# An adaLN transformer block with linear attention on one core: a new order of work on all five engines, one tile of the first norm moved from GpSimd to ScalarE, and waits left out

## The chip, the core and the metric

The kernel runs on one core of a Trainium2 chip. Its time is the device time of one execution in microseconds; every time below is in microseconds unless marked ns. The engines are TensorE (PE in the profile, PEld for its weight loads), VectorE (DVE), ScalarE (ACT), GpSimd (POOL) and SyncE (SP), which here only issues DMAs.

## The reference

`x` has shape (8, 1024, 128). A condition gives for each of the 8 batches six rows of 128 numbers. The block is

```python
h = _layernorm(x) * (1 + ca) + sa
x = x + ga * attn(h, ...)          # 6 layers
h = _layernorm(x) * (1 + cb) + sb
x = x + gb * ffn(h, ...)           # fp4 quantised, inner width 352
```

Each of the six layers of `attn` does, with 8 heads of 16,

```python
xn = _layernorm(x, ln1_w[i], ln1_b[i])
q, k, v = xn @ wq[i], xn @ wk[i], xn @ wv[i]
q = softmax(q, axis=-1); k = softmax(k, axis=-2)     # k over the 1024 rows
context = einsum('bhnd,bhne->bhde', k, v)
x = einsum('bhnd,bhde->bhne', q, context) @ wo[i] + bo[i] + x
xn = _layernorm(x, ln2_w[i], ln2_b[i])
hdn = xn @ w1[i]                                     # 128 -> 512
x = where(hdn >= 0, hdn, 0.01 * hdn) @ w2[i] + x
```

`ffn` rounds its input, its hidden values and its weights to a grid of 4-bit floats in blocks of 16.

## The kernel before

An **item** is one batch in one layer: 48 items, batch by batch within a layer. An item is 1024 rows, held as 8 tiles of 128x128 (`T = 8`), all in SBUF. Every engine runs a hand-written order: a function `items(v)` lists steps such as `if on(v - 3): first_mlp(v - 3, 0)`, and is called for v = 0, 1, 2 and so on. The engines meet only through semaphores, so v on one engine is not the same time as v on another. A software pipeline results: while TensorE makes `product_k(v)`, it also works on the context of item v-1, the attention of v-2, and the MLP of v-3 to v-5.

The steps of one item, in the order of the data:

- `bn1_rows`, `moments1` (VectorE), `root1` (GpSimd) and `normalise1`: mean and variance of each row, then the normalised tiles. Of the 8 tiles GpSimd makes the first `POOL_TILES = 3` (L1758), ScalarE the other 5 (L861).
- `block_n` (VectorE, L1198) turns 32x32 squares; `send_n` and `fetch_n` (SyncE) move the squares through DRAM, which completes a transpose; `first_norm_t` (ScalarE, L817) applies the layer's scale. Item 0 (`FIRST_N = 1`) uses TensorE transposes in place of this way, and so do items 0 to 2 (`FIRST = 3`) for q and k.
- `product_k` (L556) writes the PSUM pair `S1`, `product_q` (L568) the pair `S0`, both fp32.
- `max_k`, `exp_k`, `block_k` (L1207), `send_k`, `fetch_k` for k; `max_q`, `shift_q`, `exp_q`, `sum_q`, `inverse_q`, `normalise_q` (GpSimd, L1791), `block_q` (L1184), `send_q`, `fetch_q` for q.
- `product_z` (L577, 16 fp32 instructions), `affine_z` (VectorE, L1228), `context` (L585, two instructions), `mask_context` (VectorE, L1233), `context_out` (L591, two), `bias_context` (VectorE, L1241), `attend` (L598, 16 fp32), `add_attention` (VectorE). Each of these waits for the one before it.
- `bn2_rows`, `moments2`, `root2`, `normalise2`, `second_norm_high`, `second_norm_low` (GpSimd): the second norm, split into two fp16 halves that a transposing DMA turns (`turn_hi`, `turn_lo`).
- `first_mlp(i, n)` for n = 0 to 7: three fp16 matmuls of 512 columns each (L612 to L614) into one of two PSUM banks in turn; `copy_hidden` (ScalarE, L880) empties the bank with the activation. `hidden_high` (ScalarE, L889) and `hidden_low` (GpSimd, L1785; for items 46 and 47 VectorE) split the hidden values.
- `second_mlp(i, t)` for t = 0 to 7: twelve fp16 matmuls of 128 columns each (L627 to L629); `add_mlp` (VectorE) adds the result to x.

In items 10 to 44 VectorE does one further step per v, `round_weights` or `prepare_gates`, for the feed-forward part at the end. That part works in 16 units of half a batch, in `ffn_phase(w)`; its first units are woven by hand into v = 48 to 53.

At the start the front norm of all batches (`front_stats`, `front_root`, `front_hat`, `front_rows`) and the splitting of the MLP weights (`prepare_weights`) are woven into v = 0 to 5, and TensorE runs filler matmuls (`keep_warm`, L522) between the products.

Of the kernel before, what the change touches and what calls it, by code (L numbers as in the profile page):

```python
# [37 lines left out]
def adaln_block(nc, x, ln1_w, ln1_b, wq, wk, wv, wo, bo, ln2_w, ln2_b, w1, w2,  # L38
# [23 lines left out]
    POOL_TILES = 3  # L62
    FIRST_N, FIRST = 1, 3
# [6 lines left out]
    with ctx:  # L70
# [208 lines left out]
        def _(sp):  # L279
# [169 lines left out]
        def _(pe):  # L449
# [110 lines left out]
            def product_q(i):  # L560

                pe.wait_ge(norm1_t_ready, i + 1)
                pe.wait_ge(wq_ready, 16 * (i // B + 1))
                after(pe, q_shifted, i)
# [16 lines left out]
            def context(i):  # L581
                pe.wait_ge(z_t_ready, i + 1)
                pe.wait_ge(wv_ready, 16 * (i // B + 1))
                w = wv_s[:, i // B % 2 * D:i // B % 2 * D + D]
                nc.tensor.matmul(S1[:, 0:D], w, z_t, start=True, stop=True).then_inc(ctx_done, 1)  # L585

            def context_out(i):
                pe.wait_ge(ctx_t_ready, i + 1)
                pe.wait_ge(wo_ready, 16 * (i // B + 1))
# [11 lines left out]
            def first_mlp(i, n):  # L601
# [14 lines left out]
            def second_mlp(i, t):  # L616
# [3 lines left out]
                if t % TH == 0:  # L620
                    pe.wait_ge(weights_ready, 2 * DEPTH)
# [39 lines left out]
            def product_gate(u, t):  # L661
                pe.wait_ge(f_x_q_t_ready, u + 1)
# [4 lines left out]
            def product_up(u, t):  # L667
                pe.wait_ge(f_x_q_t_ready, u + 1)
# [4 lines left out]
            def turn_hidden(u, t):  # L673
                if u == 0:
                    pe.wait_ge(x_ready, 2 * ITEMS - 1)
                pe.wait_ge(f_hid_q_ready, u + 1)
# [7 lines left out]
            def product_down(u):  # L684
# [3 lines left out]
                pe.wait_ge(f_x1_ready, u + 1)  # L688
# [29 lines left out]
            def items(v):  # L718
                if v == 0: turned_bias_rows()
                if v == 0: hidden_bias_cols()  # L720
                if v == 0: output_bias_rows()
                if v == 0: keep_warm(mlp0_bank, 18)
                if v == 0: turn_first_n(0)
                if on(v - 2): context_out(v - 2)
                if v == 2: keep_warm(mlp0_bank, 10)
                if v == 3: keep_warm(mlp0_bank, 16)
                if on(v - 4): first_mlp(v - 4, 6)
                if on(v - 4): first_mlp(v - 4, 7)
                if v == 51: product_gate(1, 0)
                if on(v - 2): attend(v - 2)  # L730
                if on(v - 5): second_mlp(v - 5, 5)
                if on(v - 5): second_mlp(v - 5, 6)
                if v == 50: turn_rows(0)
                if v == 52: turn_hidden(0, 0)
                if on(v): product_k(v)
                if v == 1: turn_first_k(0)
                if v == 3: turn_first_q(2)
                if on(v - 5): second_mlp(v - 5, 7)
                if v == 49: turn_weights()
# [4 lines left out]
                if v == 51: product_up(1, 1)  # L744
                if v == 51: product_gate(1, 2)
                if on(v): product_q(v)
                if v == 0: keep_warm(mlp0_bank, 30)
                if v == 0: prepare_bounds()
                if v == 0: keep_warm(S0, 14, q_shifted, 1)
                if v == 0: prepare_downs()  # L750
                if v == 1: keep_warm(mlp0_bank, 20)
                if v == 1: turn_first_q(0)
                if v == 2: keep_warm(mlp0_bank, 20)
                if v == 3: keep_warm(mlp0_bank, 14)
                if on(v - 3): first_mlp(v - 3, 0)
                if on(v - 3): first_mlp(v - 3, 1)
                if on(v - 4): second_mlp(v - 4, 0)
                if on(v - 3): first_mlp(v - 3, 2)
                if on(v - 3): first_mlp(v - 3, 3)
                if v == 50: product_gate(0, 1)  # L760
                if on(v - 4): second_mlp(v - 4, 1)
                if v == 51: product_up(1, 2)
                if on(v - 4): second_mlp(v - 4, 2)
                if on(v - 1): product_z(v - 1)
                if v == 1: turn_first_k(1)
                if v == 2: turn_first_q(1)
                if v == 1: keep_warm(mlp0_bank, 10)
# [1177 lines left out]
```

## Time and profile before

| | |
|---|---|
| runs | 1197.34, 1201.46, 1201.83; median 1201.46 |
| profiled execution | 1198.31, span 1196.6, mean granted TensorE clock 0.981 of full |
| TensorE busy | 1130.7 (94% of the span) |
| VectorE busy | 1074.4 (90%) |
| ScalarE busy | 1035.2 (87%) |
| GpSimd busy | 1091.4 (91%) |

The shares are over the whole span, of which some 120 us are the start, 830 us the items in their steady pace and 240 us the end. A matmul record ends later than the next begins, since matmuls are pipelined and their ends are modelled: distances between starts tell more than durations. Records of VectorE and ScalarE also overlap the next by some 0.1 us.

### The profile page before, as it was taken

How to read it: one execution, taken by the hardware profiler on the slowest of the kernel's cores; microseconds unless marked ns; L12 is line 12 of the kernel's file. 1: busy time of each engine (PE TensorE's matmuls, PEld its weight loads, DVE VectorE, ACT ScalarE, POOL GpSimd, SP SyncE). 2: the span in 40 equal slices, each digit the busy share in tenths (PEclk: the TensorE clock that was granted, in tenths of full speed). 3: DMA queues.
4: the chain of work that ended last, by engine and by line, in shares of the span. 5: the costliest groups of instructions: out<-in, count | busy, mean ns of one | idle time of the engine just before them, and what ended most of it. 6: DMA issues, size and time to landing. Idle time of an engine off the chain costs nothing.

```text
span 1196.6 us, 30119 instructions
## 1 busy us (share of the span) xinstructions
PE 1130.7 (94%) x9722; PEld 865.7 (72%) x9722; DVE 1074.4 (90%) x2885; ACT 1035.2 (87%) x1776; POOL 1091.4 (91%) x920
## 2 busy tenths in 40 slices
PE   7787999999999999999999999999999988999996
PEld 5575777777777777777778777777787755565664
DVE  7899989989999999999999999999987589999972
ACT  5687999999999999999999999999999886767662
POOL 4889999999999999999999999999999988999762
PEclk8798999999999999999999999999999999999998
DMA  8121877777667776687776776766777420110000
GB/s 308 36 71 53 234 187 224 195 195 223 193 195 214 196 216 194 180 224 187 216 201 197 216 206 183 221 190 204 208 193 218 108 71 18 36 37 36 18 19 36
DMA packets 213864, 190.22 MB, mean 159 GB/s; under 512 B 113392, under 2 KB 192080, under 8 KB 213712
## 3 DMA queue, kind: packets, MB, share of 16 engines
q1 hardware_dynamic: 213712, 188.31, 55.3%
q8 instruction: 81, 1.33, 0.5%
q14 instruction: 71, 0.58, 0.2%
HBM read 87.06 MB, written 76.02 MB: 136 GB/s over the span
## 4 chain that ended last, share of the span: by engine, by line
PE 50%; POOL 24%; issue 15%; DVE 6%; ACT 2%; DMA 1%; SPq 1%; DVEq 0%; POOLq 0%; ACTq 0%
POOL hidden L1785 10%; POOL rows_split L1777 4%; PE pair_mlp L556 4%; PE pair_mlp L577 4%; PE pair L598 4%; PE pair L568 4%; PE ring_pair L612 3%; PE ring_pair L614 3%; PE ring_pair L613 3%; PE mlp L696 3%; PE pair_mlp L670 3%; POOL arena L1758 2%; POOL arena L1791 2%; PE pair_mlp L681 2%; PE mlp L629 2%
## 5 line engine op out<-in xcount | busy, mean ns | idle before, releaser
L1785 POOL TENSOR_TENSOR hidden<-hidden 128x2048 f16<-128x2048 f32 x92 | 376.3, 4090 | 0.0
L880 ACT ACTIVATE hidden<-ring_pair,hidden_bias 128x512 f32<-128x512 f32 x384 | 245.6, 686 | 26.1 <-PE ring_pair L614 26.0
L889 ACT ACTIVATE hidden<-hidden 128x2048 f16<-128x2048 f32 x96 | 183.3, 1909 | 19.9 <-PE mlp L629 16.1
L1097 DVE BATCH_NORM_STATS2 bn<-x_all 128x6 f32<-128x128 f32 x896 | 184.2, 278 | 5.3 <-POOL x_all L1737 2.0
L1711 POOL TENSOR_TENSOR rstd<-ve,minus_half 128x8 f32<-128x8 f32 x104 | 170.7, 1641 | 0.0
L850 ACT ACTIVATE arena<-x_all,nmr,rstd 128x128 f32<-128x128 f32 x384 | 157.7, 494 | 0.0
L612 PE MATMUL ring_pair<-arena,halves 128*128 128x512 f16 x384 | 146.0, 380 | 3.4 <-ACT hidden L880 1.7
L614 PE MATMUL ring_pair<-arena,halves 128*128 128x512 f16 x384 | 146.0, 380 | 0.0
L613 PE MATMUL ring_pair<-arena,halves 128*128 128x512 f16 x384 | 146.0, 380 | 0.0
L627 PE MATMUL mlp<-halves,hidden 128*128 128x128 f16 x768 | 135.9, 219 | 1.4 <-issue 1.4
L627 PE MATMUL pair_mlp<-halves,hidden 128*128 128x128 f16 x768 | 136.0, 219 | 0.0
L628 PE MATMUL pair_mlp<-halves,hidden 128*128 128x128 f16 x768 | 136.0, 219 | 0.0
L629 PE MATMUL pair_mlp<-halves,hidden 128*128 128x128 f16 x768 | 136.0, 219 | 0.0
L629 PE MATMUL mlp<-halves,hidden 128*128 128x128 f16 x768 | 135.9, 219 | 0.0
L628 PE MATMUL mlp<-halves,hidden 128*128 128x128 f16 x768 | 135.9, 219 | 0.0
L1777 POOL TENSOR_TENSOR rows_split<-arena,rows_split 128x1024 f16<-128x1024 f32 x48 | 103.9, 2164 | 0.3 <-ACT rows_split L870 0.3
L598 PEld LDWEIGHTS pair<-small,arena 128*128 128x128 f32 x768 | 95.1, 195 | 10.6 <-DVE small L1241 4.2
L1791 POOL TENSOR_TENSOR arena<-arena,q_rec 128x1024 f32<-128x1024 f32 x48 | 93.9, 1956 | 6.9 <-DVE q_rec L1177 6.4
L598 PE MATMUL pair<-small,arena 128*128 128x128 f32 x768 | 95.9, 279 | 3.0 <-DVE small L1241 3.0
L861 ACT ACTIVATE arena<-x_all,nmr,rstd 128x128 f32<-128x128 f32 x240 | 97.8, 498 | 1.1 <-POOL nmr L1750 1.1
L556 PE MATMUL pair_mlp<-arena,layer_w 128*128 128x512 f32 x192 | 96.2, 624 | 1.4 <-ACT arena L811 1.4
L577 PE MATMUL pair_mlp<-arena 128*128 128x128 f32 x752 | 94.3, 279 | 3.0 <-DMA arena<-k_away 2.7
(206 smaller groups left out, 3144.5 us busy)
## 6 DMA issues: line engine op xcount, KB each, us to landing
n_away<-all_blocks SPq DMA_DIRECT2D x47, 512.0 KB, 3.0
norm_raw<-n_away SPq DMA_DIRECT2D x188, 128.0 KB, 3.2
k_away<-all_blocks SPq DMA_DIRECT2D x45, 512.0 KB, 2.8
q_away<-all_blocks SPq DMA_DIRECT2D x45, 512.0 KB, 3.3
arena<-k_away SPq DMA_DIRECT2D x180, 128.0 KB, 3.5
arena<-q_away SPq DMA_DIRECT2D x180, 128.0 KB, 3.6
x_all<-in_L_attn_x SPq DMA_DIRECT2D x8, 512.0 KB, 5.5
x_in<-in_L_attn_x SPq DMA_DIRECT2D x8, 512.0 KB, 4.0
```

The lines of the kernel that those rows point to most:

```text
L598: last = nc.tensor.matmul(tile(S0, t), tile(q_prob_t, t), ctx_o, start=True, stop=True)
L612: nc.tensor.matmul(ring[n % 2], hi, rows_hi, start=True, stop=False)
L613: nc.tensor.matmul(ring[n % 2], lo, rows_hi, start=False, stop=False)
L614: nc.tensor.matmul(ring[n % 2], hi, rows_lo, start=False, stop=True).then_inc(hidden_done, 1)
L627: nc.tensor.matmul(o, rows_hi, hi, start=(c == 0), stop=False)
L628: nc.tensor.matmul(o, rows_hi, lo, start=False, stop=False)
L629: last = nc.tensor.matmul(o, rows_lo, hi, start=False, stop=(c == HC - 1))
L880: act.activation(hidden_t[:, c * W + h * HALF:c * W + (h + 1) * HALF], ring[n % 2], ACT.Prelu, bias=hidden_bias[:, b:b + 1], scale=HIDDEN_ ...
L889: act.activation(half_rows(hidden_hi, h), half_rows(hidden_t, h), ACT.Copy).then_inc(hidden_hi_ready, 1)
L1097: last = nc.vector.bn_stats(bn[:, 6 * t:6 * t + 6], src(t))
L1711: return pool.tensor_tensor(rstd[:, 0:tiles], ve[:, 0:tiles], minus_half[:, 0:tiles], ALU.pow).then_inc(rstd_ready, 1)
L1785: pool.tensor_tensor(half_rows(hidden_lo, h), half_rows(hidden_t, h), half_rows(hidden_hi, h), ALU.subtract).then_inc(hidden_lo_ready, 1)
```

## The change

`POOL_TILES` goes from 3 to 2, so GpSimd normalises two tiles and ScalarE six. `FIRST` goes from 3 to 2: item 2's k and q go through DRAM. All `keep_warm` calls are dropped. The `items` orders of all five engines are new; in steady state `context_out` and `attend` of item v-1 now stand at the end of the same v. `second_norm_low` and `normalise_q` stand one v earlier at the end of GpSimd's order, `bn2_rows`, `add_attention` and `block_q` elsewhere in VectorE's, with `round_weights` and `prepare_gates` behind `bias_context`; `x_epsilon(4)`, `x_rows(6)` and `x_multiply(0)` change their place by a step or two. Waits that an earlier wait on the same engine already covers are left out. No instruction that computes is added or removed but those that follow from the two constants.

```diff
-    POOL_TILES = 3
-    FIRST_N, FIRST = 1, 3
+    POOL_TILES = 2
+    FIRST_N, FIRST = 1, 2
...
  SyncE
+                if on(v - 2): fetch_k(v - 2)
                 if on(v - 2): send_q(v - 2)
-                if on(v - 2): fetch_k(v - 2)
...
  waits, TensorE (those on VectorE, ScalarE and the other products alike)
                 pe.wait_ge(norm1_t_ready, i + 1)
-                pe.wait_ge(wk_ready, 16 * (i // B + 1))
+                if i % B == 0:
+                    pe.wait_ge(wk_ready, 16 * (i // B + 1))
...
-                after(pe, ctx_o_ready, i - 1)
...
-                pe.wait_ge(weights_ready, DEPTH)
-                pe.wait_ge(norm2_hi_ready, 16 * (i + 1))
-                pe.wait_ge(norm2_lo_ready, 16 * (i + 1))
+                if i == 0 and n == 0:
+                    pe.wait_ge(weights_ready, DEPTH)
+                if n == 0:
+                    pe.wait_ge(norm2_hi_ready, 16 * (i + 1))
+                    pe.wait_ge(norm2_lo_ready, 16 * (i + 1))
...
```

The steady part of the orders, each in one v (the steps of the start and of the end left out):

```
TensorE before: context_out(v-2)  first_mlp(v-4, 6 7)  attend(v-2)  second_mlp(v-5, 5 6)  product_k(v)
                second_mlp(v-5, 7)  product_q(v)  first_mlp(v-3, 0 1)  second_mlp(v-4, 0)  first_mlp(v-3, 2 3)
                second_mlp(v-4, 1 2)  product_z(v-1)  first_mlp(v-3, 4 5)  context(v-1)  second_mlp(v-4, 3 4)
TensorE after:  first_mlp(v-4, 6 7)  second_mlp(v-5, 4 5 6 7)  product_k(v)  first_mlp(v-3, 0)  product_q(v)
                first_mlp(v-3, 1)  second_mlp(v-4, 0 1)  first_mlp(v-3, 2)  product_z(v-1)  second_mlp(v-4, 2)
                first_mlp(v-3, 3)  context(v-1)  first_mlp(v-3, 4)  context_out(v-1)  second_mlp(v-4, 3)
                first_mlp(v-3, 5)  attend(v-1)

VectorE before: add_attention(v-4)  inverse_k(v-3)  bn2_rows(v-4)  moments2(v-4)  add_mlp(v-7,1)  max_k(v-2)
                block_n(v-1)  max_q(v-2)  shift_q(v-2)  bn1_rows(v)  moments1(v)  EXTRA STEP  affine_z(v-3)
                sum_q(v-2)  mask_context(v-3)  inverse_q(v-2)  bias_context(v-3)  block_k(v-2)  block_q(v-2)
                add_mlp(v-6,0)
VectorE after:  add_mlp(v-7,1)  block_q(v-3)  moments2(v-4)  max_k(v-2)  block_n(v-1)  max_q(v-2)  shift_q(v-2)
                bn1_rows(v)  affine_z(v-3)  moments1(v)  mask_context(v-3)  block_k(v-2)  bias_context(v-3)
                EXTRA STEP  inverse_k(v-2)  sum_q(v-2)  inverse_q(v-2)  add_attention(v-3)  add_mlp(v-6,0)
                bn2_rows(v-3)

ScalarE before: copy_hidden(v-5, 0 1)  exp_k(v-2)  copy_hidden(v-5, 2 3)  normalise2(v-4,0)  exp_q(v-2)
                normalise2(v-4,1)  copy_hidden(v-5, 4 5)  second_norm_high(v-4)  first_norm_t(v-1)
                hidden_high(v-5,0)  copy_hidden(v-5, 6 7)  normalise1(v)  hidden_high(v-5,1)
ScalarE after:  normalise2(v-4,0)  copy_hidden(v-5, 2)  normalise2(v-4,1)  copy_hidden(v-5, 3)
                second_norm_high(v-4)  exp_q(v-2)  copy_hidden(v-5, 4 5)  hidden_high(v-5,0)  copy_hidden(v-5, 6)
                first_norm_t(v-1)  copy_hidden(v-5, 7)  normalise1(v)  hidden_high(v-5,1)  copy_hidden(v-4, 0)
                exp_k(v-1)  copy_hidden(v-4, 1)

GpSimd before:  normalise_q(v-3)  second_norm_low(v-5)  normalise1(v-1)  hidden_low(v-6,0)  root2(v-4)
                hidden_low(v-6,1)  root1(v)
GpSimd after:   normalise1(v-1)  hidden_low(v-6,0)  root2(v-4)  hidden_low(v-6,1)  root1(v)
                second_norm_low(v-4)  normalise_q(v-2)
```

At the start `output_bias_rows` moves from ahead of `turn_first_n(0)` to behind `product_k(0)`, `fold_weights` on ScalarE from v = 0 to v = 1, `weight_bounds(0)` on VectorE from v = 1 to v = 2, and `prepare_scales` to a later place in v = 3.

## Rows read from the trace of the kernel before

**Rows 1.** Busy time by stretch: PE, PEld, DVE, ACT, POOL, PEclk, DMA share, GB/s.

```profile
100.00:150.00 50.00, 45.47 (x349) 33.64 (x348) 47.10 (x128) 42.89 (x71) 45.95 (x38) 0.90 0.58 163
...
300.00:500.00 200.00, 199.65 (x1908) 156.15 (x1906) 190.58 (x513) 190.82 (x304) 196.22 (x165) 1.00 0.71 201
```

**Rows 2.** Order of time, TensorE, product_k of items 5 and 47: start, length.

```profile
139.81 1.94 PE L556 MATMUL pair_mlp<-arena,layer_w 128*128 128x512 f32 x4
...
914.83 1.94 PE L556 MATMUL pair_mlp<-arena,layer_w 128*128 128x512 f32 x4
```

**Rows 3.** Order of time, TensorE, 519 to 528 us.

```profile
519.34 2.00 PE L577 MATMUL pair_mlp<-arena 128*128 128x128 f32 x16
521.18 0.38 PE L612 MATMUL ring_pair<-arena,halves 128*128 128x512 f16 x1
...
522.47 0.38 PE L585 MATMUL pair_mlp<-small,layer_w 128*128 128x128 f32 x2
522.69 0.22 PE L627 MATMUL pair_mlp<-halves,hidden 128*128 128x128 f16 x1
...
524.03 0.44 PE L591 MATMUL pair_mlp<-layer_w,small 128*128 128x128 f32 x2
524.31 0.38 PE L612 MATMUL ring_pair<-arena,halves 128*128 128x512 f16 x1
...
525.60 1.95 PE L598 MATMUL pair<-small,arena 128*128 128x128 f32 x16
527.39 0.22 PE L627 MATMUL mlp<-halves,hidden 128*128 128x128 f16 x1
```

**Rows 4.** Order of time, VectorE and one weight load, 502 to 527 us.

```profile
502.26 1.52 DVE L1421 TENSOR_TENSOR f_w<-f_w,x_in 128x560 f32<-128x560 f32 x1
503.70 0.34 DVE L1228 TENSOR_SCALAR small<-pair_mlp,ln_cols 128x128 f32<-128x128 f32 x1
...
504.09 0.30 PEld L585 LDWEIGHTS pair_mlp<-small,layer_w 128*128 128x128 f32 x2 [0.57 <-DVE small L1228]
...
520.88 1.18 DVE L1284 TENSOR_SCALAR x_in<-mod_out 128x512 f32<-128x512 f32 x1
521.98 0.34 DVE L1228 TENSOR_SCALAR small<-pair_mlp,ln_cols 128x128 f32<-128x128 f32 x1
...
524.51 0.35 DVE L1241 SCALAR_TENSOR_TENSOR small<-pair_mlp,cols,bo_rows 128x128 f32<-128x128 f32 x1 [0.41 <-PE pair_mlp L591]
524.78 1.23 DVE L1207 STREAM_TRANSPOSE all_blocks<-arena 128x1024 f32<-128x1024 f32 x1
526.15 1.25 DVE L1184 STREAM_TRANSPOSE all_blocks<-arena 128x1024 f32<-128x1024 f32 x1
```

**Rows 5.** Order of time, GpSimd: its three tiles of one first norm.

```profile
528.20 1.31 POOL L1758 TENSOR_SCALAR arena<-x_all,rstd,nmr 128x128 f32<-128x128 f32 x3
```

**Rows 6.** Order of time, ScalarE, 529 to 535 us.

```profile
529.24 2.05 ACT L861 ACTIVATE arena<-x_all,nmr,rstd 128x128 f32<-128x128 f32 x5
531.43 1.91 ACT L889 ACTIVATE hidden<-hidden 128x2048 f16<-128x2048 f32 x1
533.86 1.34 ACT L880 ACTIVATE hidden<-ring_pair,hidden_bias 128x512 f32<-128x512 f32 x2 [0.52 <-PE ring_pair L614]
```

**Rows 7.** DMAs of q: KB, median from issue to landing; four issues in time.

```profile
q_away<-all_blocks SPq DMA_DIRECT2D x45, 512.0 KB, 3.3
...
arena<-q_away SPq DMA_DIRECT2D x180, 128.0 KB, 3.6
...
516.76 2.15 SPq L352 DMA_DIRECT2D arena<-q_away  x4
```

**Rows 8.** Order of time, TensorE, product_k of item 1.

```profile
56.43 3.78 PE L556 MATMUL pair_mlp<-arena,layer_w 128*128 128x512 f32 x4
```

**Rows 9.** Order of time, the end of the items: SyncE and VectorE.

```profile
934.97 2.24 SPq L369 DMA_DIRECT2D arena<-k_away  x4
...
942.83 0.35 DVE L1228 TENSOR_SCALAR small<-pair_mlp,ln_cols 128x128 f32<-128x128 f32 x1 [5.78 <-PE pair_mlp L577]
```

More of the change, by code:

```diff
@@ L784, in items @@
                 if v == 51: product_gate(2, 0)
-                if v == 51: product_up(2, 0)
-                if v == 51: product_gate(2, 1)
+                if on(v - 3): first_mlp(v - 3, 2)
+                if on(v - 1): product_z(v - 1)
+                if on(v - 4): second_mlp(v - 4, 2)
+                if on(v - 3): first_mlp(v - 3, 3)
+                if v == 50: product_gate(0, 1)
+                if on(v - 1): context(v - 1)
+                if on(v - 3): first_mlp(v - 3, 4)
+                if on(v - 1): context_out(v - 1)
+                if on(v - 4): second_mlp(v - 4, 3)
+                if v == 50: product_up(0, 1)
+                if v == 50: product_gate(0, 2)
+                if on(v - 3): first_mlp(v - 3, 5)
+                if on(v - 1): attend(v - 1)
             for v in range(ITEMS + 5):
@@ L875, in copy_hidden @@
                 act.wait_ge(hidden_done, PIECES * i + n + 1)
-                act.wait_ge(scales_ready, 1)
+                if i == 0 and n == 0:
+                    act.wait_ge(scales_ready, 1)
                 if c == 0:
@@ L1598, in items @@
                 if v == 53: hidden_max(1)
+                if on(v - 3): block_q(v - 3)
+                if on(v - 4): moments2(v - 4)
+                if v == 51: x_scaled(0)
+                if v == 51: x_shifted(0)
+                if v == 51: x_moments(2)
+                if v == 51: x_max(0)
+                if v == 51: x_scale(0)
+                if v == 51: x_inverse(0)
+                if v == 51: x_lift(0)
+                if v == 51: x_lower(0)
                 if on(v - 2): max_k(v - 2)
+                if v == 2: weight_bounds(0)
                 if v == 2: output_bias()
-                if v == 49: x_rows(1)
-                if v == 49: x_moments(1)
                 if on(v - 1): block_n(v - 1)
                 if on(v - 2): max_q(v - 2)
+                if v == 4: prepare_weights(0, range(0, 3))
+                if v == 5: prepare_weights(1, range(0, 3))
+                if on(v - 2): shift_q(v - 2)
+                if v == 48: x_rows(0)
+                if v == 49: x_rows(1)
+                if on(v): bn1_rows(v)
                 if v == 2: prepare_bounds()
-                if on(v - 2): shift_q(v - 2)
-                if on(v): bn1_rows(v)
-                if v == 2: front_stats(4)
-                if v == 5: prepare_weights(1, range(0, 3))
+                if on(v - 3): affine_z(v - 3)
                 if on(v): moments1(v)
@@ L1879, in items @@
                 if v == 0: front_root(1)
-                if on(v - 3): normalise_q(v - 3)
-                if v == 4: front_root(6)
-                if on(v - 5): second_norm_low(v - 5)
-                if v == 49: gate(1)
                 if on(v - 1): normalise1(v - 1)
@@ L1909, in items @@
                 if v == 51: x_divide(0)
+                if on(v - 6): hidden_low(v - 6, 1)
+                if v == 48: gate(1)
+                if v == 49: gate(2)
+                if v == 51: x_multiply(0)
                 if on(v): root1(v)
-                if v == 2: front_root(4)
+                if v == 3: front_root(5)
+                if v == 3: front_rows(4)
+                if on(v - 4): second_norm_low(v - 4)
+                if v == 47: gate(0)
+                if v == 50: x_root(1)
+                if on(v - 2): normalise_q(v - 2)
                 if v == 4: front_root(7)
@@ L1915, in _ @@
                 items(v)
-            x_multiply(0)
             x_root(2)
```

244 lines of the change are left out of this document (101 added, 143 removed).

## The prediction

> **What bounds the kernel now.** I read the busy time by stretch first, then the order of time of each engine over one item in the middle, then the start and the end. Between 300 and 500 us the fp32 and fp16 products keep TensorE busy 199.65 of 200 us at full clock, GpSimd 196.2, ScalarE 190.8, VectorE 190.6 [rows 1]: four engines within 5% of one another, so none can be read as the bound from its share. The pace is in the starts of `product_k`: item 5 starts at 139.81, item 47 at 914.83 [rows 2], 42 intervals of 18.45 us. These 775 us are two thirds of the span of 1196.6.
>
> One item on TensorE [rows 3]: the records tell starts well, ends less well, so I cost a group by the distance to the next group's start. `product_z` stands behind a `second_mlp` tile and takes 521.18 - 519.34 = 1.84. `attend`, 16 fp32 instructions like it, stands behind a `first_mlp` group and takes 527.39 - 525.60 = 1.79. `context` behind `first_mlp` takes 0.22, its twin `context_out` behind `second_mlp` 0.28. An fp32 group that starts behind a 128-column product so costs about 0.055 us more than one behind a 512-column product, once per group. Two `first_mlp` groups lie between `context_out` and `attend`: 525.60 - 524.31 = 1.29, 0.645 each; two `second_mlp` tiles between `context` and `context_out`: 524.03 - 522.69 = 1.34, 0.67 each. `product_k` I take at 1.94 less the 0.16 by which such records reach into the next group (2.00 for 1.84 of `product_z`): 1.78 [rows 2, 3]. One item is then 8 x 0.645 + 8 x 0.67 + 1.78 + 1.84 (k, q) + 1.84 + 1.79 (z, `attend`) + 0.22 + 0.28 = 18.27. So TensorE's own work is 18.27 of 18.45, TensorE is the bound, and the 0.18 above it in the mean are stalls. One is seen whole [rows 4]: a `round_weights` step of 1.52 us on VectorE stands ahead of `affine_z` (L1228), which starts at 503.70 where a shorter step (item after) lets it start early enough; TensorE's weight load for `context` then sits idle 0.57.
>
> **The change part by part.** (1) *TensorE's order.* In steady state `product_q` moves from behind `second_mlp` 7 to behind `first_mlp` 0, `product_z` from behind `second_mlp` 2 to behind `first_mlp` 2, `context_out` from behind `second_mlp` 4 to behind `first_mlp` 4. `product_k` stays behind a `second_mlp` tile, `context` and `attend` behind `first_mlp`. 3 x 0.055 = 0.17, floor 18.27 - 0.17 = 18.10.
>
> (2) *First norm.* GpSimd gives up one of three tiles: 1.31 us for three [rows 5], so 0.44 less. It was busy 98% of the time [rows 1]; what it needs falls to about 17.6. ScalarE gets it: five tiles in 2.05 [rows 6], 0.41 more at most. In a period of 18.27 ScalarE waits 0.24 behind the five tiles (531.43 less 529.24 less 1.95, its records overlapping by 0.1) and 0.62 ahead of 533.86 (1.81 after 531.43) [rows 6]: work 17.4, new 17.8. That fits under 18.10 with 0.3 over.
>
> (3) *VectorE's order.* Between two `affine_z` (503.70 and 521.98) lie 18.28 us, of which 0.42 wait for `context_out` (like the 0.41 in front of 524.51), 0.14 for q's probabilities (as between 524.78 with its 1.23 and 526.15), and 1.10 are an extra step (1.18 less the overlap of 0.08) [rows 4]: work 16.6. With an extra step, 17.7; with the longest (1.52, 1.44 net), 18.05. The extra step moves from ahead of `affine_z` to behind `bias_context`, where nothing on TensorE waits for it at once. So the stall of rows 4 has no cause left, and even the longest step fits, with 0.05 to spare.
>
> (4) *What comes close.* `context` to `context_out` had 1.34 us of `second_mlp` between, now one `first_mlp`: 0.22 + 0.645 = 0.87 from start to start. In this time `context` must end, `mask_context` run and the weights be loaded. The record of 504.09 says how fast that goes: `affine_z` starts 503.70 and the weight load starts 0.39 later; a group whose load was late begins about 0.11 later in effect; and VectorE's answer to a finished pair comes 0.42 after its start (524.03 to 524.51, less 0.06 for standing behind a short product) [rows 3, 4]. `mask_context` is 0.06 shorter than `affine_z`, so 0.33. Sum 0.42 + 0.33 + 0.11 = 0.86 against 0.87: no stall if VectorE is already waiting, which it is when its extra step is short; a stall of its lateness otherwise. From `context` to `attend` there are 0.87 + 0.22 + 0.67 + 0.645 = 2.40; needed are 0.42, the mask 0.20, `block_k` 1.15 (1.23 less the overlap), `bias_context` to the load 0.40, and 0.11: 2.28. I take 0.05 per item for both: 18.15. Bounds: 18.10, and 18.35 if each long step costs what it cost before.
>
> (5) *DMA and SyncE.* `fetch_k` now goes out ahead of `send_q`, `normalise_q` follows the sum directly, `block_q` comes after the two additions, and ends some 9.9 us behind `mask_context`'s start (an estimate: the 17.7 of work less 7.8 for the steps from `moments2` to `moments1`). Then `q_away` 3.3, four fetches issued in 2.15, the last 1.6 after the first, and 3.6 to land [rows 7]: 9.9 + 3.3 + 1.6 + 3.6 = 18.4, and `attend` of this item comes 20.1 behind that mask (a period and the 2.40 less 0.42 of the last part). 1.7 over at medians. `send_n` and the two turns of the second norm follow `block_n`, `second_norm_high` and `second_norm_low` as before, and these keep their distance to their users to within a microsecond. Worth 0; if the cover goes, `attend` waits, and half of each us comes on every item, since the loop spans two.
>
> (6) *Implied waits* on all engines: passed waits cost nothing that shows; `first_mlp` has four of them and starts on the beat [rows 3]. Worth 0.
>
> Steady part: 42 x (18.45 - 18.15) = 12.6 us gained; at 18.10, 14.7; at 18.35, 4.2.
>
> (7) *The start.* All 172 filler products go, item 2 takes the DMA way (one `copy_k`, one `copy_q` less on ScalarE, two VectorE transposes of 1.16 more), the output bias rows move behind `product_k(0)`. VectorE is busy 47.1 of 50 us here [rows 1], so it is the bound and its 2.3 more count, at most 2.9 per 50 us of idle can be saved. Clock: `product_k(1)`, after a pause of TensorE, took 3.78 for what takes 1.94 later [rows 2, 8]: 1.2 instead of 2.4 GHz. Without fillers more groups do so. What VectorE waits for directly (`context`, `context_out`, `attend`) is 2.4 us more per item at half clock; three items, 7 us, if nothing hides it; hidden it is 0. On the other side the work ahead of `product_k(0)` shrinks by about 6. I take +2, bounds -4 and +8. The Trainium skill (TensorE: Matmul & The Clock Gate, section "Why this matters for your kernels") says that a pause between bursts of matmuls puts the engine back to half clock; by that rule all of items 0 to 3 are at half clock, which is my third rival below, and the row of `product_k(1)` agrees with it, since even with fillers it fell.
>
> (8) *The end.* From item 47 on VectorE stands 5.78 us in front of `affine_z(47)`, because `fetch_k` went out at 934.97, behind `send_q` [rows 9]. Now `block_k(47)` is ahead of `bias_context` and `fetch_k` ahead of `send_q`; then `product_z(47)` no longer has to wait for `block_q`, the two turns and `send_q` to be issued; I put that at 3 us. What follows, 16 equal units of the feed-forward part, is not touched. I take -3, bounds -6 and +4, as VectorE's hand order of the last items is changed throughout.
>
> Sum: -12.6 + 2 - 3 = -13.6. The profiled execution took 1198.3 us (span 1196.6 and 1.7 around it): 1184.7. The median of the runs is 3.2 above it, which gives 1187.9, so 1188.
>
> **The rivals.** (a) *VectorE becomes the bound.* It has 0.05 over in long steps; with 0.3 more per item (waits, or slower neighbours) the period is 18.35 and the sum is -4.2 - 1 = -5: 1196. For it: 35 of the 42 items have an extra step. Against: the step stands where it blocks nothing. (b) *ScalarE becomes the bound.* It now needs 17.8; if it keeps waiting 0.86 per item as before, the period is 18.6, 42 x 0.2 = 7 slower, less 1: 1207. It decides from waits of 0.65 on. Against: its waits were slack from TensorE's pace and shrink with it. (c) *The start at half clock.* All four 1.8 us groups and the two small ones double: 7.8 per item, 23 for three, if TensorE is the chain; then -15.6 + 23 = +7: 1209, slower by over 0.5% from 22 us on and no gain from 16. Against: VectorE, not TensorE, fills that time. (d) *All goes well:* 18.10, start 0, end -6: -21, 1180. (e) The reorder does nothing, since the tail of 0.055 comes from modelled ends: the starts do not depend on these; then 18.32 and 1195, counted with (a).
>
> **How the numbers follow.** My forecast 0.62 (own range 1182 to 1194), (a) with (e) 0.16, (b) 0.06, (c) 0.08, (d) 0.08. A measurement of this kernel tells 0.5%, 6 us, from no change. Faster by more (under 1195.5): forecast, (d), a third of (a): 0.75. Within 0.5%: the rest of (a), half of (c): 0.15. Slower: (b), the rest of (c): 0.10. The range 1178 to 1203 leaves out the best tenth-part of (d) and (b) with the end of (c).
>
> **What would show it.** Starts of `product_k` 18.1 to 18.2 apart with all 42 alike; `product_q` and `product_z` 1.79 instead of 1.84; no wait of TensorE for L1228; GpSimd under 98%, ScalarE at 98%. Wrong would be: waits of TensorE for `mask_context` or `bias_context` of over 0.1 per item, ScalarE without gaps at 18.3 or more, `product_k(4)` much later than 121.95, or the first unit of the feed-forward part later against item 47 than now.

## The result and the profile after

The changed kernel takes 1205.17 us, median of 7 runs (1201.43 to 1205.8), the kernel before 1200.92 beside it on the same chip. The ratio is 1.0039, with an interval of 1.0026 to 1.0052: slower by 4 us (0.4%), not faster by 13. The forecast of 1188 was wrong, and 1205.17 lies above the range of 1178 to 1203.

The head of the page of the changed kernel, its busy time between 300 and 500 us, and the starts of `product_k` of items 5 and 47 answer to [rows 1, 2]:

```profile
span 1199.6 us, 28217 instructions
PE 1108.4 (92%) x9534; PEld 851.3 (71%) x9534; DVE 1049.0 (87%) x2887; ACT 1045.5 (87%) x1822; POOL 1069.8 (89%) x872
```
```profile
300.00:500.00 200.00, 196.26 (x1903) 156.09 (x1902) 182.53 (x511) 193.26 (x314) 192.56 (x152) 1.00 0.71 202
```
```profile
141.37 1.98 PE L556 MATMUL pair_mlp<-arena,layer_w 128*128 128x512 f32 x4
...
919.19 1.94 PE L556 MATMUL pair_mlp<-arena,layer_w 128*128 128x512 f32 x4
```

TensorE has gone from 199.65 busy us in 200 to 196.26, VectorE and GpSimd have lost share as well, and only ScalarE, which got a tile, has gained. TensorE is still the busiest, but now it also stands still at times. The span divides so: up to `product_k(5)` 1.6 more than before (141.37 against 139.81; the forecast had +2), from item 47 on 1.4 less (280.4 against 281.8; the forecast had -3), and the 42 intervals between, which were to give 12.6, take 777.8 instead of 775.0.

Within these intervals the forecast's floor is there: most are 18.11 long (18.10 was worked out), so in most items TensorE still sets the pace. But some are 18.6 to 19.9. Added up over the groups of TensorE, stalls between items 5 and 47 are 17.5 us, against 7.4 to 8.1 before. Where they stand is in the list of waits between 200 and 914 us (engine and line, what it waited for: total, times, longest; L615 is the first product of `first_mlp`, L576 `product_z`):

```profile
PEld ring_pair L615 <- issue: 24.2, 33, 2.4
...
PEld ring_pair L615 <- DMA arena<-rows_split: 9.9, 5, 2.1
...
PEld pair_mlp L576 <- DMA arena<-k_away: 2.8, 3, 1.2
```

Most of the 24.2 us of the first row lie below a `product_k` that still runs and cost nothing: a weight load that waits is a stall only where the products behind it start late. Group by group, 10.9 of the 17.5 us stand ahead of `first_mlp` 0 (8 items, at most 1.79), 3.0 ahead of `product_z`, 2.4 ahead of `attend`. Nothing of this was in the list of what would make the forecast wrong: these are waits for DMAs. The transfers out of `rows_split` are the two turned halves of the second norm, which `turn_hi` and `turn_lo` bring. What the SyncE queue waited for most, first in the changed kernel, then in the one before, 200 to 914 us:

```profile
SPq L80 <- PE ring_pair L617: 131.5, 38, 3.8
```
```profile
SPq L360 <- DVE all_blocks L1207: 172.1, 39, 5.4
```

The wait of the first view has no row in the kernel before. L80 is the helper `after`, and L617 is the last product of a `first_mlp` piece, the one that counts `hidden_done`. In the code, which the change leaves alone here:

```
def turn_hi(i):
    sp.wait_ge(rows_hi_ready, i + 1)
    after(sp, hidden_done, PIECES * i)
    sp.dma_start(norm2_hi.rearrange(...), rows_hi, transpose=True).then_inc(norm2_hi_ready, 16)
```

There is one buffer of the turned norm. Item i may be turned into it only when `first_mlp` 7 of item i-1 has read it. Before the change SyncE never waited for this: it was held up by `send_k`, which waits for `block_k`, and when that had gone the buffer was free, though not for long: `turn_hi` goes out 0.7 us behind the end of `first_mlp` 7 in nearly every item. Here is one item of before, the last product of `first_mlp` 7, `product_k` and the first product of the next `first_mlp` 0 on TensorE, then SyncE:

```profile
507.12 0.38 PE L614 MATMUL ring_pair<-arena,halves 128*128 128x512 f16 x1
510.45 1.94 PE L556 MATMUL pair_mlp<-arena,layer_w 128*128 128x512 f32 x4
514.74 0.38 PE L612 MATMUL ring_pair<-arena,halves 128*128 128x512 f16 x1
...
507.77 0.34 SPq L360 DMA_DIRECT2D k_away<-all_blocks  x1
508.20 1.41 SPq L331 DMA_TRANSPOSE arena<-rows_split  x1
509.96 1.23 SPq L336 DMA_TRANSPOSE arena<-rows_split  x1
```

And two items of the changed kernel, with the same three places on TensorE, one on the beat and one that stalls:

```profile
655.73 0.38 PE L617 MATMUL ring_pair<-arena,halves 128*128 128x512 f16 x1
658.63 1.94 PE L556 MATMUL pair_mlp<-arena,layer_w 128*128 128x512 f32 x4
660.40 0.38 PE L615 MATMUL ring_pair<-arena,halves 128*128 128x512 f16 x1
...
673.84 0.38 PE L617 MATMUL ring_pair<-arena,halves 128*128 128x512 f16 x1
676.74 1.94 PE L556 MATMUL pair_mlp<-arena,layer_w 128*128 128x512 f32 x4
680.04 0.38 PE L615 MATMUL ring_pair<-arena,halves 128*128 128x512 f16 x1 [1.37 <-issue]
```
```profile
652.35 0.34 SPq L360 DMA_DIRECT2D k_away<-all_blocks  x1
656.19 1.23 SPq L331 DMA_TRANSPOSE arena<-rows_split  x1
657.51 1.26 SPq L336 DMA_TRANSPOSE arena<-rows_split  x1
658.87 1.95 SPq L369 DMA_DIRECT2D arena<-k_away  x4
...
674.31 1.23 SPq L331 DMA_TRANSPOSE arena<-rows_split  x1
675.96 2.05 SPq L336 DMA_TRANSPOSE arena<-rows_split  x1
```

From the end of `first_mlp` 7 to the start of the next `first_mlp` 0 there were 514.74 - 507.50 = 7.2 us. Now there are 660.40 - 656.11 = 4.3, since `attend` and `product_q` (1.79 and 1.84) no longer lie between, and one more `second_mlp` tile (0.67) does. Into the gap must go: the release (0.1), `turn_hi` at the queue (1.32 from issue to issue), and the landing of `turn_lo`, 2.8 at the median. That is 4.2 of 4.3. It fits at the median, and each longer landing (they run to 4.5) or second issue (675.96, 1.65 behind the first) stops TensorE. The long ones are no plain scatter. The eight items that stall stand five apart (6, 11, 16 and so on to 41), and in each of the eight a transfer of the queue that the page calls instruction (q8, 16 KB each) starts 0.97 to 2.28 us behind the issue of `turn_hi`; in the other 34 of items 2 to 43 none starts between that issue and the landing of `turn_lo`. That the one delays the other is a guess from this coincidence, and no run tried it. `fetch_k` stands behind both turns in the queue and so is late for `product_z`. The DMAs themselves have not slowed: the two turns landed in 3.5 and 2.9 us at the median before, in 2.7 and 2.8 after. The Trainium skill (DMA: Bandwidth & Descriptors, section "Anatomy of one DMA — SWDGE (gpsimd) path") says of the DMA engines that they do not wait on semaphores, and that such a wait is spent on the issuing sequencer before dispatch. The row of 131.5 us, on the queue of SyncE, agrees, and it is why the wait also delays what stands behind.

### The profile page after: what moved, and what is told of

It reads as the page before. It is cut to its first block, busy times and chain, and to the rows that moved or that the text cites. A ratio compares the mean times of both kernels' runs of the same rounds, so it can differ in the third digit from the quotient of the medians.

```text
span 1199.6 us, 28217 instructions
## 1 busy us (share of the span) xinstructions
PE 1108.4 (92%) x9534; PEld 851.3 (71%) x9534; DVE 1049.0 (87%) x2887; ACT 1045.5 (87%) x1822; POOL 1069.8 (89%) x872
## 4 chain that ended last, share of the span: by engine, by line
POOL 48%; issue 30%; DVE 13%; PE 7%; ACT 1%; DMA 0%; POOLq 0%; DVEq 0%; SPq 0%; ACTq 0%
POOL hidden L1773 28%; POOL rows_split L1765 9%; POOL arena L1746 3%; DVE ring_pair L1357 2%; DVE arena L1494 2%; PE pair_mlp L674 1%; DVE arena L1375 1%; POOL arena L1779 1%; DVE bn L1086 1%; PE mlp L700 1%; DVE arena L1372 1%; POOL shift L1754 1%; POOL ve L1753 1%; PE mlp L510 1%; POOL nmr L1760 1%
## 5 line engine op out<-in xcount | busy, mean ns | idle before, releaser
L871 ACT ACTIVATE hidden<-ring_pair,hidden_bias 128x512 f32<-128x512 f32 x384 | 257.8, 686 | 34.2 <-PE ring_pair L617 31.4
L615 PE MATMUL ring_pair<-arena,halves 128*128 128x512 f16 x384 | 146.0, 380 | 20.1 <-issue 10.0
L840 ACT ACTIVATE arena<-x_all,nmr,rstd 128x128 f32<-128x128 f32 x384 | 158.7, 499 | 5.4 <-POOL nmr L1760 5.3
L617 PE MATMUL ring_pair<-arena,halves 128*128 128x512 f16 x384 | 146.0, 380 | 0.0
L633 PE MATMUL mlp<-halves,hidden 128*128 128x128 f16 x768 | 131.3, 219 | 0.0
L631 PE MATMUL mlp<-halves,hidden 128*128 128x128 f16 x768 | 131.3, 219 | 0.0
L632 PE MATMUL mlp<-halves,hidden 128*128 128x128 f16 x768 | 131.3, 219 | 0.0
L851 ACT ACTIVATE arena<-x_all,nmr,rstd 128x128 f32<-128x128 f32 x288 | 116.0, 496 | 0.0
L1765 POOL TENSOR_TENSOR rows_split<-arena,rows_split 128x1024 f16<-128x1024 f32 x48 | 113.7, 2368 | 0.0
L599 PE MATMUL pair<-small,arena 128*128 128x128 f32 x768 | 98.4, 283 | 4.2 <-DVE small L1230 2.6
L576 PEld LDWEIGHTS pair_mlp<-arena 128*128 128x128 f32 x752 | 90.7, 192 | 13.2 <-DMA arena<-k_away 4.5
```

Source lines behind the costliest of these rows:

```text
L599: last = nc.tensor.matmul(tile(S0, t), tile(q_prob_t, t), ctx_o, start=True, stop=True)
L615: nc.tensor.matmul(ring[n % 2], hi, rows_hi, start=True, stop=False)
L631: nc.tensor.matmul(o, rows_hi, hi, start=(c == 0), stop=False)
L632: nc.tensor.matmul(o, rows_hi, lo, start=False, stop=False)
L633: last = nc.tensor.matmul(o, rows_lo, hi, start=False, stop=(c == HC - 1))
L840: last = act.activation(tile(norm2, t), x_all[:, bass.ds((i % B) * W + t * D, D)], ACT.Identity, scale=rstd2[:, t:t + 1], bias=nmr2[:, t:t ...
```

## The experiments

The theory: the wait for the single buffer, in a gap cut from 7.2 to 4.3 us, makes the stalls. The kernels ran in four sessions, each beside the kernel before, whose medians were 1199.0, 1200.1, 1200.8 and 1199.3. The times are medians; ratios are to the kernel before.

**A second buffer.** Item i then waits only for `first_mlp` 7 of item i-2:

```
+ norm2_more = sb("norm2_more", W)
- after(sp, hidden_done, PIECES * i)
+ after(sp, hidden_done, PIECES * (i - 1))     # and norm2_hi[i % 2], norm2_lo[i % 2]
```

> The changed kernel with a second buffer for the turned halves of the second norm, so that turn_hi and turn_lo of an item no longer wait for first_mlp 7 of the item before; nothing else differs. Theory 1 (the new TensorE order leaves only 4.4 us between the end of first_mlp 7 and the start of first_mlp 0 of the next item, and two transposing DMAs have to be issued and land in it): the 10.9 us of waits ahead of first_mlp 0 go, and the waits for k (3.0 us) too, because fetch_k behind the two turns is issued some 2 us earlier; about 14 us less than the changed kernel, 1191, 0.8% under the kernel before. Theory 2 (DMAs land later in this order because the queues are fuller, wherever they are issued): the waits move to other users and at least two thirds of the 17.5 us stay, 1200 to 1205.

Measured: 1184.6 us (1184.35 to 1185.94), ratio 0.988 [0.986, 0.990]. In its trace (one line is added, so 557 is 556 of before) `product_k` and the turns stand so:

```profile
142.15 1.98 PE L557 MATMUL pair_mlp<-arena,layer_w 128*128 128x512 f32 x4
903.63 1.94 PE L557 MATMUL pair_mlp<-arena,layer_w 128*128 128x512 f32 x4
...
607.03 0.34 SPq L361 DMA_DIRECT2D k_away<-all_blocks  x1
607.47 1.53 SPq L332 DMA_TRANSPOSE arena<-rows_split  x1
609.59 1.23 SPq L337 DMA_TRANSPOSE arena<-rows_split  x1
...
615.08 0.38 PE L616 MATMUL ring_pair<-arena,halves 128*128 128x512 f16 x1
```

SyncE's wait for L618 (617 of the changed kernel) is 0.4 us in all instead of 131.5. `turn_lo` goes out 5.5 us ahead of its reader, and the steady part is 903.63 - 142.15 = 761.5 us: 42 intervals of 18.13. This is the forecast's own steady part (18.15), and 1184.6 is inside its range.

**The same buffer in the old order**, as a control:

> The kernel before with the second buffer for the turned second norm, nothing else: the control for the two_buffers run. Theory 1 (the buffer matters only since the new order brought first_mlp 7 and the next first_mlp 0 close): in the kernel before some 7.4 us lie between the two and nothing waited there after the start, so within 0.3% of the kernel before, 1196 to 1202. Rival (the buffer helps any order, for instance since SyncE's later fetches go out earlier, so the change gave nothing): most of the 1.2% that two_buffers gained, 1186 to 1190.

Measured: 1200.4 us, ratio 1.001 [0.999, 1.002]. The buffer is worth nothing where the gap is 7.2 us. So it is not a gain in itself; the new order made it short.

**A longer gap instead of a buffer:** `product_q` ahead of `first_mlp` 0.

```
+ if on(v): product_q(v)
  if on(v - 3): first_mlp(v - 3, 0)
- if on(v): product_q(v)
```

> The changed kernel with product_q ahead of first_mlp 0 instead of behind it, one swap in TensorE's order. Theory 1: first_mlp 0 comes 1.8 us later against the turns, more than the longest stall seen there (1.79), so 10.9 us of waits go; product_q stands behind a second_mlp tile again and costs 0.055 us more per item, 2.3 us. Sum 8.6 us less than the changed kernel, 1196.5, 0.35% under the kernel before; the period without a stall is 18.16. If the waits ahead of first_mlp 0 are not for the turns: no gain, 1207.

Measured: 1194.6 us (1192.36 to 1198.2), ratio 0.996 [0.995, 0.997]. `first_mlp` 0 stalls 0.7 us in place of 10.9, but `product_z` now 6.8 in place of 3.0, because the turns still wait for the buffer (132.3 us) and `fetch_k` stands behind them. The interval stays 18.11: I had expected 18.16, but `product_q` stands behind `product_k` here, with 512 columns, and not behind a short product.

**The first norm's tile alone**, in the old order (`POOL_TILES = 2`), and given back in the new one (`POOL_TILES = 3`):

> The kernel before with two tiles of the first norm on GpSimd and six on ScalarE, nothing else. If TensorE's own 18.27 us per item bound the kernel before: within 0.2% of it, 1199 to 1203. If GpSimd, on which the chain that ended last ran up to about 480 us, set the pace there: up to 0.44 us less for some 18 items, 8 us less, 1193. If ScalarE has no room for the tile: up to 0.4 us more per item, 17 us, 1218.

> The changed kernel with three tiles of the first norm on GpSimd and five on ScalarE, nothing else. GpSimd's work is then 17.6 + 0.44 = 18.0 us for a period of 18.11, and it waits about 0.3 per item for q's reciprocals: if the moved tile is needed for the new pace, the period without a stall rises to some 18.3 and the time by about 8 us, to 1213. If GpSimd's waits are slack, the period stays 18.11 and the time within 2 us of the changed kernel's 1205.

Measured: 1195.3 us (ratio 0.997 [0.996, 0.998]) and 1205.3 us (1.005 [1.003, 1.007]). In the old order the tile takes the stalls around `context` (3.8 us) and 1.9 of the 2.8 in front of `product_z`: the interval is 18.27 almost throughout, 1.5 to 2.1 us of stalls are left, and the steady part is 6.1 us shorter (the start 1.9 longer). The time lies between the first two cases, since both hold in part: TensorE bounds, at 18.27, and the stalls above that were GpSimd's lateness. VectorE hands it on, though its list of waits between 200 and 910 us has none for GpSimd. The step of [rows 4] that took 1.52 us at 502.26 is the same instruction that takes 0.77 with two tiles. First GpSimd beside it in the kernel before, then GpSimd and VectorE with two tiles:

```profile
499.09 4.10 POOL L1785 TENSOR_TENSOR hidden<-hidden 128x2048 f16<-128x2048 f32 x1
```
```profile
496.45 4.08 POOL L1785 TENSOR_TENSOR hidden<-hidden 128x2048 f16<-128x2048 f32 x1
500.36 0.77 DVE L1421 TENSOR_TENSOR f_w<-f_w,x_in 128x560 f32<-128x560 f32 x1
501.05 0.34 DVE L1228 TENSOR_SCALAR small<-pair_mlp,ln_cols 128x128 f32<-128x128 f32 x1
```

Before, `hidden_low` on GpSimd ends at 503.2, 0.9 us behind the start of VectorE's step; with two tiles it ends 0.2 behind it. In both the step ends some 0.6 behind that end, and `affine_z` (L1228) follows. So GpSimd, earlier by the tile, lets go of VectorE's extra steps earlier: those of 128x512 or 128x560 elements took 0.98 to 1.52 us before and take 0.39 to 0.88 here, but for the reductions, 0.70 in both. In the changed kernel giving the tile back costs no more than its runs spread.

**With two buffers, the parts of the forecast one at a time.** First `product_z` back behind a 128-column product (`second_mlp` 2 ahead of it):

> The two_buffers kernel with product_z behind second_mlp 2 instead of ahead of it, so that its first fp32 weight load stands behind a 128-column product. If the tail is what the order gained: product_z takes 1.84 instead of 1.79, the period goes from 18.11 to 18.16 or 18.17, 2.3 us more in 42 items, 1187. If the place behind a short or a long product costs nothing: 18.11 and 1184.6.

Measured: 1189.4 us, ratio 0.992 [0.990, 0.993], 4.8 more than two buffers alone, twice what was expected (4.2 more in the steady part of the traces). Each interval is 18.23 instead of 18.11:

```profile
404.67 2.00 PE L577 MATMUL pair_mlp<-arena 128*128 128x128 f32 x16
406.51 0.38 PE L616 MATMUL ring_pair<-arena,halves 128*128 128x512 f16 x1
...
407.12 0.30 PEld L586 LDWEIGHTS pair_mlp<-small,layer_w 128*128 128x128 f32 x2 [0.29 <-DVE small L1217]
407.16 0.45 PE L586 MATMUL pair_mlp<-small,layer_w 128*128 128x128 f32 x2
407.45 0.38 PE L616 MATMUL ring_pair<-arena,halves 128*128 128x512 f16 x1
```

`product_z` takes 1.84 (1.78 to 1.79 with two buffers), the 0.055 of the forecast. The other 0.07 is at `context`, 0.29 instead of 0.22: only `first_mlp` 3 is left between the two, and `affine_z` comes 0.1 late. The term was right, and the swap made a wait beside it.

Then 172 fillers at the start again (the expectation says 178; the edit has 172, as many as before), in the places where the new order has its pauses, and all waits that the change had left out:

> The two_buffers kernel with 178 filler products at the start again, near their places of before. If the half clock at the start costs time (rival c of the prediction, 16 to 23 us, or my own 2): product_k of item 5 starts 2 to 8 us earlier than the 142.15 of two_buffers and the whole is that much shorter, 1177 to 1182. If VectorE and GpSimd fill that time anyway: product_k of item 5 within 1 us, 1184 to 1186.

> The two_buffers kernel with all the waits that the change left out as implied put back, on TensorE, ScalarE and VectorE. Passed waits cost nothing: period 18.11, 1184 to 1186. If each costs some tens of ns of a queue: first_mlp has up to three more per group and TensorE is at its floor, so the period would rise by 0.1 to 0.5 us, 4 to 20 us in all.

Measured: 1184.8 us (1183.83 to 1185.47) with the fillers, no different; `product_k(5)` starts 0.6 earlier. The granted clock did go up, as the busy time from 50 to 100 us shows, first without and then with them (the clock is the number behind POOL's):

```profile
50.00:100.00 50.00, 33.63 (x151) 26.03 (x150) 48.72 (x161) 39.30 (x76) 36.83 (x43) 0.67 0.28 81
```
```profile
50.00:100.00 50.00, 36.29 (x247) 29.70 (x248) 47.76 (x171) 38.91 (x74) 37.16 (x41) 0.87 0.26 76
```

VectorE is busy 48.7 of the 50 us in the one and 47.8 in the other: it sets this stretch, whatever the clock. With the waits back 1187.2 us (1187.12 to 1187.47), 2.6 more, above the 1184 to 1186 of the first case. Its steady part is 761.2 us, as without them, `product_k(5)` is 0.4 later and the stretch behind item 47 1.1 longer. So passed waits cost nothing per item, and a little at the ends; why there, no run shows.

**The queue order of SyncE.** If the turns must wait, can `fetch_k` go ahead of them?

```
- if on(v - 2): fetch_k(v - 2)     (first in the item)
  if on(v - 1): send_k(v - 1)
+ if on(v - 1): fetch_k(v - 1)
  if on(v - 3): turn_hi(v - 3)
```

> The changed kernel with one line of SyncE's order moved: the fetch of the k blocks stands behind its own send, ahead of the two turns of the second norm, instead of behind them. In the kernel with product_q ahead of first_mlp 0 the send went out at 596.10 and the turns at 599.93, so the fetch should go out near 598.5 and be on the queue for 2 us, and the turns, which wait for first_mlp 7, lose nothing. Theory (both waits have the turns' buffer as their source: first_mlp 0 waits for the landing itself, product_z for what stands behind the turns in the queue): product_z's stalls (3.0 us between 158 and 914) go, those of first_mlp 0 (10.9 us) stay, so about 1202 us. Rival (the DMA engines are simply more loaded): both stay, 1205 us, or the sum moves from one to the other.

> product_q ahead of first_mlp 0 on TensorE, and the fetch of the k blocks ahead of the two turns on SyncE; still one buffer of the turned second norm. Theory: the first half took 10 us of first_mlp 0's stalls and left 6.8 us at product_z, because the fetch stands behind the turns; with the fetch ahead, those go too and only attend's wait for the q blocks is left: 1187 to 1189 us, without the second buffer. Rival (the stalls are of the load of the DMA engines, and move to whichever user is next): 1193 to 1196 us.

Measured: 1262.3 us (ratio 1.052 [1.050, 1.054]) and 1198.5 us (0.998 [0.997, 1.000]). Both missed, the first by 60 us, and the second is no better than the swap of `product_q` alone (0.996). Its chain of work that ended last, over one item:

```profile
576.45 3.20 DMA arena<-rows_split
579.65 1.08 issue
580.73 0.38 PE ring_pair L615
...
589.06 0.23 PE pair_mlp L585 x2
589.32 0.07 DVE small L1221
...
589.53 1.25 DVE all_blocks L1195
590.79 3.42 DMA k_away<-all_blocks
594.23 0.30 SPq L369
...
595.52 0.43 SPq L369
596.05 3.26 DMA arena<-rows_split
```

This is a ring. The turn lands, `first_mlp` 0 and the products up to `context` run, `mask_context` and `block_k` follow on VectorE, `send_k` goes out and lands, and only then can `fetch_k` be issued, and the next turn behind it: 596.05 - 576.45 = 19.6 us, 18.84 with a shorter landing (the next turn is at 614.89), 19.8 in the mean of 42. I had judged `fetch_k` by the issue time of `send_k` in another kernel, 596.10 against a turn at 599.93, where 3.8 us hid the landing; the send itself depends on the turn. With `first_mlp` 0 moved back by `product_q` the ring is loose enough to run at 18.11, but stalls of 8.3 us come back ahead of `first_mlp` 0, because SyncE now waits 91.1 us for k's landings with the turns behind.

**`block_q` ahead of the second `add_mlp`** on VectorE, so that q leaves earlier:

```
+ if on(v - 3): block_q(v - 3)
  if on(v - 7): add_mlp(v - 7, 1)
```

> The changed kernel with block_q ahead of the second add_mlp on VectorE, so that the send of the q blocks doesn't stand behind VectorE's wait for second_mlp 7 (0.47 us) and the add (0.75 us). The q blocks leave about 1.2 us earlier. Theory: attend's stalls (2.4 us between 158 and 914, largest 0.87) go, those of first_mlp 0 stay: about 1203 us. Rival: earlier traffic of the q blocks runs beside the turns and makes first_mlp 0 wait longer: 1206 us or more.

> The changed kernel with the second buffer of the turned norm and with block_q ahead of the second add_mlp on VectorE; the fetch of the k blocks stays behind the turns. Two buffers alone gave 1184.6 us. Theory: block_q took 3 us of the changed kernel, but with two buffers attend hardly waits any more (0.2 to 0.8 us between 158 and 900), so 1183 to 1185 us, 0 to 1.5 us gained. Rival: block_q 1.2 us earlier pushes something else on VectorE late (the second add_mlp, which frees mlp's bank for second_mlp 0), and it comes out at 1187 us or more.

Measured: 1202.0 us alone (1199.42 to 1208.35; ratio 1.002 [1.000, 1.004]) and 1184.8 us with two buffers (0.986 [0.984, 0.989]). Ahead of `attend` 0.9 us of stalls are left of 2.4, and 10.9 stay ahead of `first_mlp` 0. With two buffers nothing is left to win. These two sources of stalls are separate.

All repairs together, with the fetch moved, and the tile given back beside two buffers:

> The changed kernel with all the repairs: the second buffer of the turned norm, the fetch of the k blocks ahead of the turns, and block_q ahead of the second add_mlp. Two buffers alone gave 1184.6 us with 1.4 to 3.2 us of stalls left between 158 and 900 and a period of 18.11. Theory: nothing is left to win but those, 1182 to 1185 us. Rival: the earlier transfers collide with the turns or with each other and it comes out above 1186 us.

> The changed kernel with the second buffer, and the first norm's third tile given back to GpSimd (3 tiles GpSimd, 5 ScalarE, as before the change). Theory 1 (the tile was worth 4 us in the old order because affine_z stood behind the first norm's late tile; in the new order nothing of the first norm is near the path): 1184 to 1186 us, no difference. Theory 2 (the tile was worth as much here, and the turns' stalls hid it): 1188 to 1190 us.

Measured: 1261.1 us for the first; the ring above closes here too, though the buffer is free, which shows that it is made by the queue's order alone. The second took 1188.1 us (1186.95 to 1191.44), 3.5 more than two buffers. By the time that is theory 2. By the trace it is neither: the steady part is 761.5 us, the same to 0.02, and the cost stands at the start (`product_k(5)` 1.0 later) and behind item 47 (0.9). Of the other 1.5, 1.3 is that the profiled execution of two buffers, 1185.94, was that kernel's slowest.

Starts, in us, of the pieces that matter (k(5): start of `product_k(5)`; steady: from there to `product_k(47)`; end: from there to the end of the span):

| kernel | k(5) | steady | end | span |
|---|---|---|---|---|
| before | 139.8 | 775.0 | 281.8 | 1196.6 |
| after | 141.4 | 777.8 | 280.4 | 1199.6 |
| before, two tiles on GpSimd | 141.7 | 768.9 | 281.9 | 1192.4 |
| two buffers | 142.2 | 761.5 | 280.6 | 1184.2 |
| two buffers, waits back | 142.5 | 761.2 | 281.7 | 1185.4 |
| two buffers, `product_z` behind short | 142.0 | 765.6 | 279.8 | 1187.4 |
| `fetch_k` ahead of the turns | 142.3 | 832.4 | 285.6 | 1260.3 |

## Why the prediction was wrong

**The step that failed is part (5)**, where the forecast says that `send_n` and the two turns "keep their distance to their users to within a microsecond. Worth 0". It looked at what the turns follow, the two halves written by ScalarE and GpSimd, and not at what they wait for on the other side, the release of the buffer. And it took the distance to the user as kept, though part (1) itself had taken `product_q` from in front of `first_mlp` 0, and `attend` had gone from behind `first_mlp` 7. Two numbers of before would have shown it: 7.2 us between last read and next read, and some 4.7 for release, issues and landing at the median. The new order cut the first to 4.3. The runs put the price at 16.3 us of the steady part in the traces (777.8 against 761.5), which is the 10.9, 3.0 and 2.4 us of stalls from above. In the medians, which are of two sessions, it is 20.5; the profiled execution of the changed kernel, 1201.4 us, was its fastest, 3.7 under its median, and that of two buffers its slowest, 1.3 over, which is more than the difference.

With that mended, the parts of the sum come out near: -13.5, +2.3 and -1.2 in the trace of two buffers against -12.6, +2 and -3. That makes 1185.9 for the profiled execution, where the forecast had 1184.7. The 3.2 us that it then added for the median of the runs did not come: the median of two buffers, 1184.6, lies under its profiled execution. So 1188 is 3.4 over, and that it is not more is in part luck, as the end gave less than forecast and the steady part more.

Parts (1), (3) and (4), the steady floor: right. 18.11 against 18.10, and 18.13 in the mean against 18.15. The rise of 0.055 behind a 128-column product is real, as the swap of `product_z` shows, so rival (e), that it comes from modelled ends, falls. `product_q` and `product_z` take 1.78 to 1.79, as its signs said. `context_out` waits 0.23 for `mask_context` in its weight load, which costs TensorE nothing.

Part (2), the tile: in the order before it took 6 us of stalls from the steady part. The forecast saw these stalls as VectorE's doing alone, and took the 1.52 us of its longest step as the length of that work, where about half of it was the wait for GpSimd. In the new order the tile is worth nothing per item and about 2 us at start and end.

Part (6): right per item, 1.5 us off at the ends by the traces; the medians differ by 2.6 in all.

Part (7): +2 forecast, +1.6 measured. Rival (c), a start at half clock, falls. The granted clock from 50 to 100 us did go down, from 0.90 before to 0.76 here and 0.67 with two buffers, and the fillers lifted it to 0.87. `product_k` of items 0, 1 and 2 takes 3.78, 3.78 and 2.60 us with two buffers, and 1.98, 1.88 and 1.88 with the fillers. Yet the time stayed within 0.2 us. The Trainium skill's rule in TensorE: Matmul & The Clock Gate (section "Why this matters for your kernels"), that pauses put the engine back to half clock, agrees with these rows; "all of items 0 to 3" went too far, as 0.67 is between the levels, and the clock was not on the path. Part (8): -3 forecast, -1.4 measured.

Rivals (a) and (b): neither VectorE nor ScalarE became the bound; with two buffers all four engines keep up with 18.11. In (b) 18.6 less 18.45 is 0.15, and 42 of these are 6, where it says 42 x 0.2 = 7; its 1207 moves by about 1. The slower side was forecast only through these and the clock, and not through a DMA's release.

## What to carry to other kernels

When an order is changed, work out for each single buffer the time from its last reader to its next reader, and set it against release, issues in the queue, and landing; a "follows as before" is only half of a DMA's conditions, and a wait with zero time in the trace before may be the next one to hold. A gap that fits at the median is not hidden: the longest landings come out as stalls, here 8 in 42 items. The length of a step in a trace, too, can hold a wait for another engine (1.52 for 0.77 us here), and then it does not carry over to another place in the order. In a queue that waits in order, moving a transfer ahead of another also makes the second wait for all that the first waits for, and the time of a send in the trace is no constant if the moved transfer feeds what produces it.

## What the hardware showed that was not expected

A step of `prepare_gates` on VectorE, 128x512 from one SBUF tensor, took 0.41 us in the changed kernel and 1.18 in the one before. In the changed kernel (VectorE, then GpSimd) it starts just ahead of a long GpSimd step; in the kernel before it starts inside one:

```profile
616.26 0.41 DVE L1272 TENSOR_SCALAR x_in<-mod_out 128x512 f32<-128x512 f32 x1
616.33 2.34 POOL L1765 TENSOR_TENSOR rows_split<-arena,rows_split 128x1024 f16<-128x1024 f32 x1
```
```profile
517.69 4.08 POOL L1785 TENSOR_TENSOR hidden<-hidden 128x2048 f16<-128x2048 f32 x1
```

The step of before, at 520.88 [rows 4], ends at 522.06, 0.3 behind the end of GpSimd's at 521.77; and in the changed kernel GpSimd's step takes 2.34 where its shortest is 2.13. So each seems to wait for the other to finish rather than to share. The kernel before with two tiles on GpSimd bears it out: there the order of VectorE is untouched, the steps of this kind take 0.39 to 0.48 us instead of 0.98 to 1.21, and those that start inside GpSimd's step do so only 0.06 to 0.28 us ahead of its end. The reductions among the extra steps (128x560 to 128x35) take 0.70 inside a GpSimd step and 0.72 just ahead of one, so they do not wait. The Trainium skill (SBUF — State Buffer, section "SBUF: two separate sides") says so: a VectorE instruction in a two-port mode, or with two inputs from SBUF, and one of GpSimd hold a shared port pair for a whole instruction, and the other blocks. These rows agree. In part (3) the forecast carried the 1.18 over to a new place on VectorE, where it is 0.41, and the 1.52, which is 0.73 there. So it gave VectorE less room than it has, and rival (a), with 0.05 to spare in long steps, was nearer in the forecast than in the kernel.

What also was not expected is how loosely the mean clock and the time are tied: the four executions with two buffers had 0.967 to 0.974 over the span and took 1184.35 to 1185.94 us, the four with fillers 0.981 to 0.984 and 1183.83 to 1185.47, with the same steady part to 0.6 us in the two traces.
